# Staging of x and of W_attn in the head of a pre-norm transformer layer: three x buffers on one queue, W_attn rows in pairs through one buffer

## The reference, cut to what matters

```python
def reference(x, W_attn, W_proj, U1, V1, b1, U2, V2, b2):    # x: (4, 4096, 1024) f32
    def attn(x):
        q, k, v = split(x @ W_attn)                          # W_attn: (1024, 3072), 16 heads of 64
        att = einsum('bhid,bhjd->bhij', q, k) / 8
        att = polymax(where(causal, att, -inf))              # (x^2 + 1)/1000 if x > 0, else (1 - x/100)/1000
        return einsum('bhij,bhjd->bhid', att, v) @ W_proj
    def ffn(x):
        P = x @ U1                                           # rank 256
        return (gelu(P @ V1 + b1) @ U2) @ V2 + b2
    x = x + attn(layernorm(x))
    return x + ffn(layernorm(x))
```

## Time and profile before

| | us |
|---|---|
| runs shown: median of 2 | 2119.37 |
| the two runs | 2115.95, 2122.78 |
| profiled execution: its own time | 2115.12 |
| its span on the slowest core (core 1) | 2113.4 |
| spans of the 8 cores | 2096.8 to 2113.4 |

### The profile page before, as it was taken

One profiled execution on the slowest core, in us unless ns is written; L12 is line 12 of the kernel. 1 busy time (PEld: TensorE's weight loads), 2 busy tenths in 40 slices (PEclk: granted clock), 3 DMA queues, 4 the chain that ended last, 5 costly groups with the idle time before them and its releaser, 6 DMA issues.

```text
span 2113.4 us, 22659 instructions; the slowest of 8 cores (2096.8 to 2113.4 us)
## 1 busy us (share of the span) xinstructions
PE 1292.7 (61%) x6880; PEld 467.4 (22%) x6880; DVE 1259.4 (60%) x2171; ACT 760.5 (36%) x1074; POOL 0.2 (0%) x4
## 2 busy tenths in 40 slices
PE   2332255947767777776764847766775461468886
PEld 0000022424222222111111323322221120023332
DVE  2446833334689999999996323489997233344422
ACT  0110000000467777777774000167776000033333
POOL 0000000000000000000000000000000000000000
PEclk8665578979656667777777879855666685578998
DMA  4234422020000000000002020000000443001111
GB/s 124 89 110 162 156 80 80 1 80 1 1 1 1 1 1 1 1 1 1 1 1 65 15 80 1 1 1 1 1 1 20 159 139 120 0 0 41 40 41 40
DMA packets 37590, 87.68 MB, mean 41 GB/s; under 512 B 2145, under 2 KB 7522, under 8 KB 37474
## 3 DMA queue, kind: packets, MB, share of 16 engines
q1 hardware_dynamic: 22434, 58.98, 8.7%
q10 hardware_dynamic: 15040, 27.26, 3.8%
HBM read 77.85 MB, written 8.39 MB: 41 GB/s over the span
## 4 chain that ended last, share of the span: by engine, by line
PE 41%; DVE 27%; issue 16%; DMA 11%; ACT 4%; DVEq 1%; SPq 0%; ACTq 0%
DVE poolD L772 14%; PE ps L807 5%; DMA poolD<-W_attn 5%; PE ps L738 4%; PE ps L1139 3%; PE ps L944 3%; PE ps L929 3%; PE ps L1045 3%; PE ps L639 3%; PE ps L619 3%; PE ps L661 3%; PE ps L1159 3%; DMA poolA<-x_t 2%; ACT poolD L759 2%; DVE poolD L785 2%
## 5 line engine op out<-in xcount | busy, mean ns | idle before, releaser
L759 ACT ACTIVATE poolD<-ps 128x1024 bf16<-128x1024 f32 (+3 forms) x640 | 560.3, 900 | 821.6 <-PE ps L738 644.7
L772 DVE SCALAR_TENSOR_TENSOR poolD<-poolD 128x1024 bf16<-128x1024 bf16 (+3 forms) x640 | 647.4, 1059 | 44.3 <-ACT poolD L759 23.2
L807 PE MATMUL ps<-poolD,poolA 128*64 128x512 bf16 (+3 forms) x1280 | 310.7, 470 | 228.3 <-DVE poolD L772 118.3
L738 PE MATMUL ps<-poolB,poolA 64*128 64x512 bf16 (+3 forms) x1280 | 286.3, 474 | 33.5 <-ACT poolD L764 16.2
L807 PEld LDWEIGHTS ps<-poolD,poolA 128*64 128x64 bf16 x1280 | 94.1, 119 | 420.6 <-issue 420.6
L1151 ACT ACTIVATE poolC<-ps,sb_b1s 128x512 bf16<-128x512 f32 x128 | 87.9, 688 | 117.6 <-PE ps L1139 76.6
L764 ACT ACTIVATE poolD<-ps,consts 128x256 bf16<-128x256 f32 x256 | 124.1, 485 | 0.0
L738 PEld LDWEIGHTS ps<-poolB,poolA 64*128 64x128 bf16 x1280 | 65.2, 102 | 238.0 <-issue 236.8
L445 PE MATMUL ps<-poolD,sb_onescol 128*1 128x512 bf16 x64 | 32.9, 513 | 109.3 <-DVE poolD L442 109.2
L815 PE MATMUL ps<-poolD,poolA 128*64 128x128 bf16 x512 | 86.7, 306 | 0.0
L1045 PE MATMUL ps<-poolC,poolD 128*128 128x512 bf16 x256 | 57.4, 388 | 41.2 <-DVE poolD L987 41.2
(11 more groups left out here) (100 smaller groups left out, 1149.7 us busy)
## 6 DMA issues: line engine op xcount, KB each, us to landing
poolD<-W_attn SPq DMA_DIRECT2D x40, 512.0 KB, 4.2
poolD<-x_t SPq DMA_DIRECT2D x8, 2048.0 KB, 11.1
poolA<-x_t ACTq DMA_DIRECT2D x8, 2048.0 KB, 10.2
poolC<-x_own_t SPq DMA_DIRECT2D x8, 1024.0 KB, 5.6
y<-poolC SPq DMA_DIRECT2D x4, 2048.0 KB, 6.6
poolD<-W_proj SPq DMA_DIRECT2D x8, 512.0 KB, 4.1
poolD<-U ACTq DMA_DIRECT2D x5, 512.0 KB, 4.2
poolC<-U ACTq DMA_DIRECT2D x5, 512.0 KB, 4.5
```

The lines of the kernel that those rows point to most:

```text
L738: e.matmul(o, l, r, skip_group_check=True, start=True, stop=True, tile_position=tp),
L759: e.activation(o, i, AF.Relu), inc="S")
L772: e.scalar_tensor_tensor(o, i, 0.01, i, ALU.add, ALU.mult),
L807: e.matmul(o, l, r, skip_group_check=True, start=st, stop=True, tile_position=tp),
```

## The change

The x blocks of both passes go through three buffers in turn (poolD, and two in poolA, of which the second is new), and every load of x is issued by SyncE's queue. A load now waits for the release of the block three before. In the weight loads, `stream_w` brings two 128-row pieces with one DMA of 1 MB into the whole of `wstage`, four times; each of the four waits for both casts of the one before. The work of TensorE, VectorE and ScalarE and its order are the same.

```diff
         xstage2_ = [view(poolD, 0, F32, [128, DC, 512]),
-                    view(poolA, 0, F32, [128, DC, 512])]
+                    view(poolA, 0, F32, [128, DC, 512]),
+                    view(poolA, 16384, F32, [128, DC, 512])]
...
-        relVs = [0, 0]
-        relTs = [0, 0]
+        relVs = [0, 0, 0]
+        relTs = [0, 0, 0]
         for tb in range(8):
-            xs = xstage2_[tb % 2]
-            q = "sync" if tb % 2 == 0 else "scalar"
-            b.wait(q, "V", relVs[tb % 2])
-            b.wait(q, "T", relTs[tb % 2])
-            dd = (b.dma if tb % 2 == 0 else b.dma2)(
-                xs[:, :, :], x_src[:, :, tb * 512:(tb + 1) * 512])
+            xs = xstage2_[tb % 3]
+            b.wait("sync", "V", relVs[tb % 3])
+            b.wait("sync", "T", relTs[tb % 3])
+            dd = b.dma(xs[:, :, :], x_src[:, :, tb * 512:(tb + 1) * 512])
...
-        relVs = [b.cnt["V"], b.cnt["V"]]
+        relVs = [b.cnt["V"]] * 3
         bc_free = 0
         p2_prev = {}
         for tb in range(8):
-            xs = xstage2_[tb % 2]
-            q = "sync" if tb % 2 == 0 else "scalar"
-            b.wait(q, "V", relVs[tb % 2])
-            dd = (b.dma if tb % 2 == 0 else b.dma2)(
-                xs[:, :, :], x_src[:, :, tb * 512:(tb + 1) * 512])
+            xs = xstage2_[tb % 3]
+            b.wait("sync", "V", relVs[tb % 3])
+            dd = b.dma(xs[:, :, :], x_src[:, :, tb * 512:(tb + 1) * 512])
...
         def stream_w(colbase, dst):
             b.wait("vector", "T", b.cnt["T"])
             casts = []
-            for dp in range(DC):
-                b.wait("sync", "V", casts[dp - 2] if dp >= 2 else b.cnt["V"])
-                dd = b.dma(wstage[:, dp % 2, :],
-                           w_src2[:, dp, colbase:colbase + 1024], slot=f"w{dp % 2}")
+            for dp in range(4):
+                b.wait("sync", "V", casts[-1] if casts else b.cnt["V"])
+                dd = b.dma(wstage[:, :, :],
+                           w_src2[:, 2 * dp:2 * dp + 2, colbase:colbase + 1024])
                 b.wait("vector", dd, 16)
-                casts.append(b.op("vector", lambda e, o=dst[:, dp, :],
-                                  s=wstage[:, dp % 2, :]: e.tensor_copy(o, s), inc="V"))
+                for k in range(2):
+                    casts.append(b.op("vector", lambda e, o=dst[:, 2 * dp + k, :],
+                                      s=wstage[:, k, :]: e.tensor_copy(o, s), inc="V"))
```

More of the change, by code:

```diff
@@ L449, in build_program @@
                 t_done[dc] = b.cnt["T"]
-            relVs[tb % 2] = b.cnt["V"]
-            relTs[tb % 2] = b.cnt["T"]
+            relVs[tb % 3] = b.cnt["V"]
+            relTs[tb % 3] = b.cnt["T"]
             b.wait("scalar", "T", tfence())
```

## The result

| | before | changed |
|---|---|---|
| median of the runs, us | 2116.56 | 2084.01 |
| profiled execution, its own time | 2115.12 | 2084.01 |
| span of its slowest core | 2113.4 (core 1) | 2082.4 (core 3) |
| mean span of the 8 cores | 2105.7 | 2077.5 |

The ratio is 0.9862, 95% interval 0.9828 to 0.9895: a real gain of 1.4%, inside 2%. 2079 was forecast. In some executions the cores of one die are granted a lower clock and take some per cent longer; every ratio and interval here leaves those out, a median does not.

What follows compares the result with a forecast made beforehand. It took waits for loads in the first 453 us, odd x blocks above all, as the bound. -43.5 - 5.0 + 8 = -40.5 us from the 2119.4 median gave 2079, range 2066 to 2098.

Steps and rivals of the forecast that it cites:

- Part 1: Statistics pass: odd x loads no longer waited for, a block every 12.7 us; 43.5 us less.
- both first loads late: Sign to look for: the first x load of the statistics pass and of the normalize pass both land late, meaning rival B.
- rival B: Three x loads on one queue share the engines, first blocks 10.5 and 5.3 us later; 2100 us in all; chance 0.07.
- Part 2: Start of the normalize pass: x block 0 no longer shares with block 1, so it lands sooner; 5.0 us less.
- Part 3: stream_w: four 1 MB steps with nothing beside them, a call 25.7 us; three calls cost 8 us more.
- T: Landing time of one 1 MB weight load in stream_w, taken as 5.15 us.
- step T + 1.46: One stream_w step in us: landing T, 0.09 to the cast, two casts, 0.06 to the next issue.
- Rival A: stream_w: 1 MB loads nearly pay for themselves, T about 4.74, costing 3.5 us; 2074 us in all; chance 0.20.
- The rule that the prediction set beside it: Weight loads: a DMA takes 2.0 us plus bytes at 436 GB/s, 4.4 us for 1 MB; the forecast didn't use it.
- Rival C: stream_w takes back the 48.5 us gained elsewhere if T reaches 8.5 us; 2131 us at T = 9.5; chance 0.03.
- Rival D: Odd loads already partly hidden or the queue can't keep up, both passes paced by loads; 2114 us; chance 0.04.
- The clause that the attention keeps its length: Everything behind 453 us only shifts; the prediction is wrong if the attention changes its length.

Runs made afterwards that it cites:

- e3: Changed kernel, but in both passes SyncE waits for block 0 to land before issuing blocks 1 and 2; ratio to before 0.9839.
- e4: Changed kernel with two x buffers instead of three, all x loads still on SyncE's queue; ratio to before 0.9844.
- e6: e4 with the normalize pass's odd x blocks back on ScalarE's queue; mean wait before its first multiplication 19.1 us, where e4 has 12.7.
- e2: Kernel before with only the weight loads changed to 1 MB pairs through one buffer, x as before; ratio to before 1.0063.
- e7: Changed kernel with loads issued as early as buffers allow, statistics blocks 1 and 2 after block 0 lands, W_attn in eight pieces through three slots; ratio to before 0.9628.

## Why the prediction was right, and where its sizes were off

The time was inside the range and the verdict inside 2%, but the sum said -40.5 us and the medians show 32.6, the stages 32.7, the profiled pair's slowest cores 31.0. The forecast of 2079 missed by only 5 us where the sum missed by 8: it started from 2119.4, the median of two runs, and the median of ten is 2116.6. That part is luck. Point by point:

*Part 1, the statistics pass: mechanism right.* Core 1, from which all its rows came, went from 146.5 to 103.1 us in that pass, 43.4 less where 43.5 was forecast (42.7 from L466 of block 0 to that of block 7, as the forecast counted). What was wrong was to take core 1 for the kernel. The mean core won 40.2, and the core that is slowest now, core 3, had waited for only 35.0 us (the earlier trace rows show 42.4 on core 1). Nor did that wait alone make core 1 the slowest: core 5 had waited 46.1 us and ended 7 us before it. A term that differs between cores has to be read on all of them.

*Part 1, the first load: a term left out.* The text reckoned with block 0 at 14.9 as before. It came 3.0 us later, since the loads behind it on its own queue take part of the rate (e3, e4). By the prediction's own sign, both first loads late (13.49 and 13.73 us on core 3), this is rival B, but in a mild form: B put 10.5 us on it.

*Part 2, forecast -5.0, measured -1.6.* The first multiplication was to start some 9 us after its load; the mean core waited 12.8, and only core 2 came near, with 9.7. "On one queue I expect them in order" holds for the most part: e6 against e4 gives 6.4 us to the single queue, where 5.3 was worked out. Two things took it back: 1 MB of later blocks still goes ahead (e3), and with all cores in step the same two-queue load takes 19.1 us instead of 14.4 (e6). So the step that failed is the comparison with 13.93 us, a landing among cores whose neighbours stood 7 us apart. The pair in the earlier trace rows was also thin evidence for "does not slow it": its first piece landed after 3.88 us where the lone one before it took 3.67, a sign of little at 512 KB, while behind 2 MB blocks the first came 2.2 to 2.8 us later than alone (changed kernel against e3). The Trainium skill ("DMA: Bandwidth & Descriptors", section on queues, rings and completion order) states ring order for one DMA engine; the trace agrees with the direction, while the MB that ran ahead shows that it is no order for whole transfers.

*Part 3, forecast +8, measured +6.1* (7.0 in e2). T was 4.9 to 5.1 instead of 5.15, and the step T + 1.46 was exact. Rival A needed 4.74, which only the fastest landing reached. The rule that the prediction set beside it (Trainium skill, "DMA: Bandwidth & Descriptors", anatomy of one DMA) is given there for DMAs issued by GpSimd. These are issued by SyncE, and the trace doesn't agree: its 4.4 us for 1 MB lie below the lowest landing, 4.7.

Together the sizes missed by 7.8 us: 3.3 in part 1, 3.0 for the first load, 3.4 in part 2, and 1.9 the other way in part 3.

*Rival C* needed landings of 8.5 us; the highest was 5.7 in the changed kernel and 6.0 in e2. *Rival D* is excluded by one wait for x in each pass, on all eight cores. The clause that the attention keeps its length held: 1078.0 before and 1078.7 changed.

## What to carry to other kernels

A DMA stands in the order of the engine whose queue issues it: an issue behind compute instructions on ScalarE starts when they are done, whatever buffers are free (block 1 at 28.45 us in the earlier trace rows), and moving it to a queue without compute was worth the whole gain here, while a third buffer was worth nothing. A wait written as "everything so far" (`b.cnt["V"]` read when the list is written) holds loads back that have a free buffer; taking such waits away, with one more slot for the weights and without the 1 MB loads, brought some 50 us more (e7). And in a program of eight cores, removing a wait of different length on each core brings the cores into step (e6: all within 2.3 us): read each term on every core, and expect the loads that follow to take longer.

## What the runs showed of the hardware that I had not expected

- Two 2 MB loads issued together on two queues took 19.1 us to deliver the first, on one queue 12.7, alone 10.6 (mean waits in the normalize pass of e6, e4 and e3).
- The third of three 2 MB loads issued in a row held SyncE's queue for about 5.5 us at the start of the changed kernel, where the issue of the first two took 0.4 to 0.6 each.
- TensorE's clock does not come back at a fixed time. In the Q projection of the changed kernel core 0 still stood at 1.2 GHz 8 us after its first matmul (at 417.7), core 1 was at 2.4 GHz 4.3 us after its own (at 420.2; PEclk is the third number from the end). The three cores that were back within 5 us take 91.5 to 92.3 us for that stage, the five that were not take 93.8 to 94.1. Core 0:

```profile
422.00:424.00 2.00, 1.05 (x26) 0.88 (x26) 1.29 (x2) 0.00 (x0) 0.00 (x0) 0.50 0.00 0
424.00:426.00 2.00, 2.00 (x6) 0.68 (x5) 0.00 (x0) 0.00 (x0) 0.00 (x0) 0.50 0.00 0
```

Core 1:

```profile
424.50:426.50 2.00, 1.25 (x28) 0.88 (x29) 1.20 (x2) 0.00 (x0) 0.00 (x0) 1.00 0.00 0
```
